# One attention-and-experts layer on one core: GpSimd rotates the queries four tiles at a time, scatters go five to a turn, and routing steps move

## The reference

```python
xn = _layernorm(x, axis=-1)
# attention: 16 heads of 16, one shared key and value head, window of 64 positions
q, k = apply_rope(q, 8), apply_rope(k, 8)      # the first 8 of 16 dims of each head
attn = softmax(q @ k.T * scale + mask);  attn_out = (attn @ v) @ Wo + bo
# experts: 64 of them, 4 per token, and 2 shared ones
_, topk_idx = top_k(xn @ router_w + router_bias, 4)
routed = sum over 4 experts of comb * ((silu(xn @ wg) * (xn @ wu)) @ wd)
return x + attn_out + (routed + shared)
```

## Time and profile before

| what | value |
|---|---|
| median of 3 runs | 364.16 us (363.85 to 364.17) |
| the profiled execution | 364.63 us, span 363.3 us, mean granted clock 0.987 |
| busy over the span | PE 93%, PEld 69%, DVE 69%, POOL 69%, ACT 50% |
| chain that ended last | PE 70%, DVE 17%, issue 5%, ACT 5% |
| turns 1 to 15 (first maxima of turn 1 to those of turn 15, VectorE) | 43.38 to 146.04 us |

### The profile page before, as it was taken

How to read it: one execution, slowest core, us unless ns; L and a number is a source line. 1 busy time by engine, 2 the same in 40 slices (tenths; PEclk the granted TensorE clock), 3 DMA queues, 4 the chain that set the end, 5 groups by cost and what they waited for, 6 DMA issues and landing times.

```text
span 363.3 us, 8649 instructions
## 1 busy us (share of the span) xinstructions
PE 337.3 (93%) x2711; PEld 250.7 (69%) x2711; DVE 250.7 (69%) x721; ACT 181.7 (50%) x343; POOL 251.7 (69%) x506
## 2 busy tenths in 40 slices
PE   6978779899999999999999999999999999999982
PEld 3776546666665665589999999999975456655572
DVE  4778788988999997556456545444476376668686
ACT  2677378797688786454555555555442101110100
POOL 6467388878778777425666667778884777777774
PEclk9989899999999999999999999999999999999998
DMA  8950235645496567689988764587974344444444
GB/s 253 230 148 1 63 104 153 199 146 163 140 254 168 163 200 214 199 249 255 351 289 259 246 197 155 189 255 253 328 261 154 98 120 130 131 125 122 130 130 130
DMA packets 73036, 66.81 MB, mean 184 GB/s; under 512 B 9053, under 2 KB 68701, under 8 KB 72993
## 3 DMA queue, kind: packets, MB, share of 16 engines
q1 hardware_dynamic: 66433, 49.30, 45.8%
q0 software_dynamic: 6144, 16.79, 14.8%
q10 hardware_dynamic: 416, 0.18, 0.3%
HBM read 36.78 MB, written 29.23 MB: 182 GB/s over the span
## 4 chain that ended last, share of the span: by engine, by line
PE 70%; DVE 17%; issue 5%; ACT 5%; DMA 1%; POOL 1%; SPq 1%; DVEq 0%; POOLq 0%; ACTq 0%
PE bank L665 17%; PE bank L604 15%; PE bank L690 10%; PE bank L624 7%; PE bank L639 5%; PE bank L418 4%; DVE xall L1102 3%; PE bank L406 2%; PE bank L555 2%; PE bank L487 2%; DVE xall L1339 2%; PE bank L530 1%; ACT xall L861 1%; DVE xall L1096 1%; DMA wdn<-edges 1%
## 5 line engine op out<-in xcount | busy, mean ns | idle before, releaser
L1517 POOL DMA_INDIRECT xs_d<-spare,slot_i x64 | 63.7, 996 | 24.9 <-issue 7.3
L1609 POOL DMA_INDIRECT wall<-y_d,y_row x64 | 62.7, 980 | 24.9 <-issue 18.9
L665 PE MATMUL bank<-xall,spare 128*128 x508 | 63.8, 278 | 0.0
L1293 DVE TENSOR_TENSOR spare<-bank,spare 64x512 f32<-64x512 f32 (+1 forms) x64 | 44.1, 690 | 28.2 <-ACT spare L910 27.3
L665 PEld LDWEIGHTS bank<-xall,spare 128*128 128x128 f32 x508 | 59.4, 192 | 2.1
L1544 POOL COPY spare<-wall 128x256 f32 x127 | 49.1, 408 | 17.0 <-PE bank L665 9.1
L604 PE MATMUL bank<-xnT,xall 128*128 128x512 f32 x128 | 57.3, 594 | 0.0
L923 ACT ACTIVATE spare<-bank 128x512 f32<-128x512 f32 (+1 forms) x62 | 33.7, 593 | 28.0 <-PE bank L690 18.6
L861 ACT ACTIVATE xall<-bank 98x1024 bf16<-98x1024 bf16 x32 | 32.9, 1027 | 19.3 <-PE bank L437 17.7
L604 PEld LDWEIGHTS bank<-xnT,xall 128*128 128x128 f32 x128 | 24.1, 190 | 25.2 <-issue 24.4
L886 ACT ACTIVATE xall<-bank 128x512 f32<-128x512 f32 x16 | 9.5, 597 | 59.6 <-PE bank L604 59.6
(11 more groups left out here) (174 smaller groups left out, 635.3 us busy)
## 6 DMA issues: line engine op xcount, KB each, us to landing
y_d<-spare SPq DMA_DIRECT2D x31, 512.0 KB, 4.1
wall<-in_wg SPq DMA_DIRECT2D x16, 256.0 KB, 3.4
wall<-in_wu SPq DMA_DIRECT2D x16, 256.0 KB, 4.3
wdn<-in_wd SPq DMA_DIRECT2D x16, 256.0 KB, 4.5
spare<-xs_d SPq DMA_DIRECT2D x32, 128.0 KB, 3.5
small<-xs_d SPq DMA_DIRECT2D x32, 128.0 KB, 3.6
wall<-in_x SPq DMA_DIRECT2D x4, 512.0 KB, 5.4
base_d<-spare SPq DMA_DIRECT2D x16, 128.0 KB
```

The source lines that it names most:

```text
L665: ins = pe.matmul(up_bank_of(G)[:, j * P:(j + 1) * P], wcur[i % NW][:, c * 2 * F:(c + 1) * 2 * F], x_half[c][:, bass.ds(o, P)], start=c == ...
L1293: ins = dve.tensor_tensor(hT[G % 2][half, 0:n], up_bank_of(G)[F:P, 0:n], sg[0:F, 0:n], ALU.mult)
L1517: pool.indirect_dma_start(out=xs_d, out_offset=bass.IndirectOffsetOnAxis(ap=slot_i[:, T, k:k + 1], axis=0), in_=x_n[b][:, t, :], in_offset ...
L1609: pool.indirect_dma_start(out=yk[:, T, k, :], out_offset=None, in_=of, in_offset=bass.IndirectOffsetOnAxis(ap=y_row[:, T, k:k + 1], axis=0 ...
```

## The change

The parts, in the words of the code:

- **Rotation.** `rotate(lo, hi)` treats tiles lo to hi-1 with four instructions. Tiles 0 to 3 are still rotated one by one in the opening. Tiles 4 to 7 are rotated at the head of turn 1, all four instructions in a row ahead of that turn's scatters; tiles 8 to 11 between the scatters of turn 5, tiles 12 to 15 between those of turn 9. `roped_with(T)` is the value of `roped` that tile T waits for. The sine and cosine constants hold each value twice, so that the inner run is 8 elements.
- **Scatters.** Five in turns 2, 3, 4, 6, 7, 8 and from 10 on, four in turns 0, 1, 5 and 9: the 64th comes in turn 13.
- **Routing steps.** The step of `lifted` and `slots` is split: one step now lifts both halves, the next two give one half of the slots each. The table has four places instead of three: the new third stands before `place(T)`, the fourth between `place(T)` and `near(T+1)`.
- **Early stack of tile 1.** `stack(1,1)` stands ahead of `totals` on TensorE and before the sixth query's copy on ScalarE; `near(1)` directly behind `place(0)`. `cast(3,0)` moves from ScalarE's turn 1 to the end of its turn 0.
- **`expert_row()`** stands ahead of `place(13)` on TensorE.

The diff, cut to what the prediction speaks of:

```diff
-    ROUTE = ((1, 1, 1), (1, 0, 1))
-    route_at = lambda T: ROUTE[T] if T < len(ROUTE) else (0, 0, 2 - T % 2 if T < 12 else 1)
+    ROUTE = ((1, 1, 0, 1), (1, 1, 0, 0), (0, 0, 1, 1), (0, 0, 1, 0), (0, 0, 1, 1), (0, 0, 1, 0), (0, 0, 1, 1), (0, 0, 1, 0),
+             (0, 0, 1, 1), (0, 0, 0, 1), (0, 0, 1, 1), (0, 0, 1, 1))
+    route_at = lambda T: ROUTE[T] if T < len(ROUTE) else (0, 0, 0, 1)
...
-    SCATTERED_AT = lambda T: 6 if T in (NT - 4, NT - 3) else 4
+    SCATTERED_AT = lambda T: 5 if T in (2, 3, 4, 6, 7, 8) or T > 9 else 4
+    roped_with = lambda T: T + 1 if T < TPB else TPB + T // TPB
...
# TensorE
             if T == 0:
+                stack(1, 1)
                 totals()
...
-            if T + 1 < NT:
+            if 0 < T < NT - 1:
                 stack(T + 1, 1)
...
+            if T == EXPERT_ROW:
+                expert_row()
             place(T)
...
# ScalarE
-            if T + 2 < NT:
+            if T + 2 < NT and T != 1:
                 cast(T + 2, 0)
...
+            if T == 0:
+                stack(1, 1)
...
             if T == 0:
+                cast(3, 0)
                 act.wait_ge(s["c32"], 16)
...
# VectorE
-            place(T)
             for _ in range(steps[2]):
                 next(route, None)
-            if T + 1 < NT:
+            place(T)
+            if T == 0:
+                near(1)
+            for _ in range(steps[3]):
+                next(route, None)
+            if 0 < T < NT - 1:
                 near(T + 1)
...
# GpSimd
+        def rotate(lo, hi):
+            pool.wait_ge(s["proj_q"], hi)
...
+            pool.tensor_tensor(a, x12, over(k32["cos"]), ALU.mult)
             yield
...
         for T in range(NT):
...
-            pieces = rotate(T + TPB) if T < NT - TPB else iter(())
+            if T == 1:
+                rotate_whole(TPB, 2 * TPB)
+            pieces = rotate(T + 3, T + 3 + TPB) if T in (TPB + 1, 2 * TPB + 1) else iter(())
```

More of the change, by code:

```diff
@@ L59, in layout_constants @@
     part = np.arange(P)
-    rows = lambda a: np.ascontiguousarray(a.reshape(TPB, P, ROT).transpose(1, 0, 2).reshape(P, TPB * ROT))
+    rows = lambda a: np.ascontiguousarray(np.repeat(a.reshape(TPB, P, 1, ROT), 2, 2).transpose(1, 0, 2, 3).reshape(P, TPB * 2 * ROT))
     f32 = {
@@ L216, in build @@
     qtok = [r[:, :, 0:SROWS].rearrange("p h (c d) -> p h c d", d=HD) for r in qrow]
-    rope = [ar.take(H * 2 * ROT).rearrange("p (h i d) -> p h i d", h=H, i=2) for _ in range(2)]
+    rope = [r.take(TPB * H * 2 * ROT).rearrange("p (t h n) -> p t h n", t=TPB, h=H) for r in (early, ar)]
     rest = ar.take(H * HD).rearrange("p (h d) -> p h d", d=HD)
@@ L749, in tensor @@
                 weigh(T - 1, 1)
-            if T == EXPERT_ROW:
-                expert_row()
             if 1 < T < NT - 1:
@@ L847, in cast @@
                     act.wait_ge(s["q_T"], 2 * (T - 2) + 2)
-                act.wait_ge(s["roped"], T + 1)
+                act.wait_ge(s["roped"], roped_with(T))
             else:
@@ L1216, in routing @@
                                   starts[:, i, :].unsqueeze(1).to_broadcast([P, 8, E]), ALU.add).then_inc(s["rank_read"], 1)
+            yield
+            for i in range(2):
+                ts = slice(8 * i, 8 * i + 8)
                 dve.wait_ge(s["rank_read"], i + 1)
@@ L1474, in prepare_k @@
             x1, x2 = k[:, :, 0:ROT], k[:, :, ROT:2 * ROT]
-            cs = k32["cos"].rearrange("p (t d) -> p t d", d=ROT)
-            sn = k32["sin"].rearrange("p (t d) -> p t d", d=ROT)
+            cs, sn = [k32[n].rearrange("p (t d) -> p t d", d=2 * ROT)[:, :, 0:ROT] for n in ("cos", "sin")]
             pool.tensor_tensor(krope[0], x1, cs, ALU.mult)
@@ L1567, in gpsimd, with rotate_whole @@
         pool.wait_ge(s["c32"], 16)
-        def rotate_whole(T):
-            for _ in rotate(T):
+        def rotate_whole(lo, hi):
+            for _ in rotate(lo, hi):
                 pass
-        rotate_whole(0)
+        rotate_whole(0, 1)
         prepare_k(0)
-        rotate_whole(1)
+        rotate_whole(1, 2)
         prepare_k(1)
         prepare_k(2)
-        rotate_whole(2)
-        rotate_whole(3)
+        rotate_whole(2, 3)
+        rotate_whole(3, 4)
         prepare_k(3)
```

25 lines of the change are left out of this document (12 added, 13 removed).

## The result

The changed kernel takes 371.89 us (median of 4 runs, 369.69 to 373.08); the kernel before, run beside it, 364.17 (363.85 to 365.61). The ratio is 1.0206, with a 95% interval from 1.0175 to 1.0237: slower, by about 2.1%. The profiled execution took 371.16 us, its span is 369.9 (363.3 before). The forecast was 368.2 in a range from 362.8 to 372.0.

The account below looks back on a forecast made before the run. TensorE bounds the expert blocks; the turns, with no engine full, decide. Late rotations put `place(15)` 4.4 us later, the hand-over returns 0.4: 364.16 + 4.0 = 368.2 us, range 362.8 to 372.0.

Parts of the forecast that it names:

- Turns 0 and 1: Start of the turns on VectorE: 3.2 us won, `place(1)` at 47.4 instead of 50.56.
- The rotation of tiles 4 to 7: On GpSimd: 1.03 us per 512-element instruction, 0.63 per 256; 3.4 us in all against 6.3 for sixteen instructions.
- The scatters: On GpSimd, 1.27 us apart: turn 0's four end at 50.3, the rotation at 53.8.
- Behind the stall: From the first rotation's end at 53.8, through the cast ending at 54.7, to `place(2)` at 59.0 (before 58.19).
- rival D: Worse than the sum: GpSimd and VectorE port contention, 0.5 to 1 us a rotation, plus slow TensorE after stalls; 371 to 372; 15%.
- Turns 3 to 5 and 7 to 9: Steps ahead of `place` give little back: turns of 7.1, 8.5 and 7.1 us, then 7.7, 7.2 and 6.1.
- Second and third rotation: Late on GpSimd, ending at 86.05 and 116.9: `place(6)` at 91.0 (before 88.09), `place(10)` at 121.6 (before 116.79).
- The hand-over: After `place(15)`: the 64th scatter issues in turn 13, so SP's first load of rows stops waiting; 0.4 us won.
- A: The moves win: GpSimd scatters 1.0 us apart (deciding sign: under 1.1), 0.8 per 512-element instruction; 362.8 us; 15%.
- C: Gain and loss cancel: unseen slack eats the second stall; 364.2 us; 8%.
- B: No rotation is late at all, so only the loop over TensorE and ScalarE counts; 358.5 us; 5%.

Follow-up runs that it names:

- the run with idle matmuls: The changed kernel plus 24, 8 and 14 matmuls that nothing reads while TensorE waits in turns 2, 6 and 10: 368.94 us.
- six ahead: The change with tiles 4 to 6 rotated before turn 0's scatters, then one tile a turn: 359.38 us; second run, routing steps behind `place` again: 361.27 us.
- GpSimd's part alone: The kernel before with only the change's GpSimd batches, tables and scatter plan, no early stack or moved routing steps: 371.45 us.
- batches in time: The change with tiles 4 to 6 rotated before turn 0's scatters, 7 between turn 1's, the others whole at heads of turns 5 and 9: 364.41 us.
- single tiles in time: Same rotation places as batches in time, but four instructions per tile and the semaphore raised after each tile: 359.06 us.

## Why the prediction was right, and what was mis-sized

The mechanism and the side are as forecast: `place(1)` came earlier and three rotations held ScalarE at the casts of tiles 4, 8 and 12, for 6.6, 4.4 and 4.2 us (4, 3 and 4 forecast). The size of the loss was not: 7.7 us against 4.0, so that the time lies 3.7 above the forecast, 0.1 below the top of the range. Between the two profiled executions the loss is 6.6: that of the change is 0.7 below its median, that of the kernel before 0.5 above its own.

*Turns 0 and 1.* Forecast `place(0)` 39.95 and `place(1)` 47.4; measured 38.74 and 45.66. The 6.9 between them is 0.5 better than my 7.45. Of the 3.2 us to be won up to `place(1)` 2.6 lay behind `place(0)` and came as 3.1. Of the 1.8 by which `place(0)` is earlier than before, at most my 0.6 is `stack(1,1)`; the rest goes with the opening's clock, which was 1.00 in this execution and down to 0.50 in that of the kernel before. That is luck, and it hid 1.2 us of what the sum had missed: with the opening as forecast this execution would have taken 372.4 us (an estimate, 371.16 + 1.21), outside the range.

*The rotation of tiles 4 to 7.* An instruction of 512 elements took 1.26 us, not 1.03, and one of 256 0.72, not 0.63: 3.95 for the rotation against 3.4. The term was mis-sized by 0.55 us a rotation. The Trainium skill, page GPSIMD Engine Reference, section 3.1, by whose quarter I had priced 1.12, was nearer than my line through the rows and also low. The new products took 0.46 us for 128 elements and 1.26 for 512, which is 2.1 ns an element and 0.19 besides (worked out from these two), and a quarter of a longer instruction takes a quarter of that part too.

*The scatters.* Spacing 1.27 as taken: from 53.24 to 78.21 twenty in a row, all but the one of 1.86 us. In turn 0 the first two took 1.19 and 1.23, so that the four took 5.3 us instead of 5.0. The rotation ended at 53.08 (forecast 53.8). The times of the queue are right within a few tenths, but since `place(1)` came 1.7 early, the stall is longer than forecast: 13.3 us against 11.6 in stretch 1–2.

*Behind the stall.* From the rotation's end to `place(2)` I had 5.2; it took 5.9. For the second rotation 4.95 and 5.94. With the stalls filled it is 5.2 and 4.9. So this is the clock, which I had priced in rival D alone and left out of the sum; the run with idle matmuls gives nearly 3 us for it in all. `place(2)` at 59.0 and `place(5)` at 81.9 (59.0 and 81.7 forecast) are right to 0.2 only because an early opening and a longer stall cancelled.

*Turns 3 to 5 and 7 to 9.* 23.0 and 21.0 us, against 22.7 and 21.1. That a step ahead of `place` gives little back was right; over all turns it gives nothing, by the two runs six ahead. VectorE's list is moved, and a wait behind `place`, for the weighting that `output` reads, grows instead: 2.5 us in two waits before, and now (us in total, times, longest):

```profile
DVE xall L1134 <- PE bank L532: 5.2, 7, 1.9
```

The idle time on the cast of tile 3 is gone, as forecast.

*Second and third rotation.* The mixed groups took 8.7 us (8.15 and 8.4 forecast). `place(6)` came at 92.85 (91.0), `place(10)` at 124.2 (121.6), `place(15)` at 156.6 (153.8).

*The hand-over.* 0.6 given back, forecast 0.4: 213.9 us behind `place(15)` before, 213.3 after.

From `place(0)` to `place(15)` I had 113.85 us and measured 117.9. GpSimd's queue has no pause between the first rotation and the second, so the 4.0 missing add up along it: 1.4 is the rotations' length (0.55, 0.55 and 0.3); 1.0 the slow clock between the second rotation's end and `place(6)` (the 0.7 behind the first is not directly on this path); 1.0 the nineteen scatters between the two, which took 25.1 us instead of 24.1, 0.9 of it in the one of 1.86; 0.5 where the third group starts, 2.2 us later than forecast with `place(9)` 1.7 later; 0.3 the turns behind `place(10)`. The stretch 6–9 gives 0.2 back.

*The rivals.* A fell at its own point: spacing 1.27. C fell with the second stall, which no slack ate. B, "no rotation is late at all", had 358.5 and is what the run six ahead shows, at 359.4: the loop count behind it was sound, and the kernel can have it by another plan. D has the number measured, 371 to 372, but its two parts went apart. Its clock is real. Its port contention is small in the change, where VectorE's `leave` took 0.42 on average and the first rotation ran while VectorE stood idle: three other VectorE instructions took 0.5 to 0.75 longer in turns 5 and 9, and one scatter 0.9. (Nor did each side hold up the other in the earlier trace rows: VectorE's product took the 1.23 that its like take everywhere, and only GpSimd's add was held.) The contention grows as soon as VectorE works beside the rotations. It is most of the loss with GpSimd's part alone, and with batches in time it costs 3.5 us: 322.4 from `place(0)` to the end against 318.9 with single tiles, 2.1 and 2.0 of it in the stretches 2–5 and 6–9.

What costs most in the change is thus neither the moves nor the length of the merged instructions, but the place and the one release: four rotations that the first cast waits for as one, behind four scatters, with 7 us of idle time ahead of them. Put right, these give 7.5 us (batches in time); the length of the instructions is then worth another 5.4 by the medians (single tiles in time). The fastest versions here, single tiles in time (359.06) and six ahead (359.38), are 1.3 to 1.5% faster than the kernel before and some 3.4% faster than the change.

## What to carry to other kernels

Merging instructions saves their fixed cost, and moves the first result to the end of the last: count what the first reader waits for, not the busy time of the engine, and look what another engine does beside the longer instructions. Before moving work earlier on one engine, look where the next thing it will ask for is made, and make that ahead in the producer's own idle time; here either step alone was worth nothing, and both together 1.3%. A stall on TensorE costs more than its length, so add what the rows show of the clock behind it.
